# A gated transformer block on one core: first FFN product between values and scores, the weight fold inside layer one, batch two's input by transposes, second FFN matrix quantised after the RELU low halves

## The chip, the cores and the metric

The kernel runs on one core of one Trainium2 chip. The metric is the device time of one execution in microseconds (us).

## The reference, cut to what matters

```python
xn = _layernorm(x, axis=-1)                   # x: 8 batches x 512 rows x 256 columns
# attention branch
q, k, v = (gelu(xn @ W1 + b1) @ W2 + b2 for each of q, k, v)
scores = einsum('bid,bjd->bij', q, k) / sqrt(256 * 512) * tril
s = layernorm(einsum('bij,bjd->bid', scores, v)) * ln_w + ln_b
# ternary FFN branch
Wq = clip(round(W / (mean(abs(W)) + EPS)), -1, 1)         # for both matrices
g = silu(relu(xn @ Wq1.T + b1) @ Wq2.T + b2)              # 256 -> 1024 -> 256
out = x + s * g
```

## The kernel before

One program per engine, each with its order written out by hand and joined by semaphores. Every engine runs eight batches: batch 0 as straight code with the preparation woven in (`first=True`), batches 1 to 6 mostly as a hardware loop, the last as straight code again. So the places named below are a position in an engine's list, and a wait on one engine holds everything behind it on that engine.

Each fp32 product is made of fp32r products of a high half and a low half: ACT rounds a tile to its high half, DVE (for v POOL) subtracts it from the full value and so makes the low half, and PE multiplies hi by hi, lo by hi and hi by lo. For GELU and RELU, ACT applies the function twice, once into the high half and once in place in PSUM (lines 423/424 and 441/442), and DVE subtracts (`g_lo`, line 594, and `r_lo`, line 670).

PE's order in a batch:
- layer one, six products of 6 matmuls (`ORDER`), from the transposed normalised input `xT`;
- K: z = the folded matrix W2q W2k applied to gelu(k), two products;
- V: four groups of matmuls of 256 columns;
- D: one product of two matmuls with `e`, which makes a per-row term `d` that enters the scores; DVE reads it with four instructions (line 647);
- F1: the FFN's first matrix, eight products of 4 matmuls;
- S: the scores, four products;
- Y0 (tiles 0 and 1) and Y1 (tile 2): the second FFN matrix, which needs all eight `r_lo` (`r_split`);
- O: scores times v; Y2 (tile 3); then the next batch.

Y0, Y1, O and Y2 are called so below; K(i) is the first K product of batch i. The PSUM banks are used in a ring: the table `AT_...` gives each result its place, place modulo 8 is the bank, and `claim` makes PE wait until the result eight places earlier has been read.

DVE's order in a batch behind the r_lo: scale the scores (`s_scale`) and make their low halves, `xT_lo` of the next batch, add the bias to Y0 and Y1, statistics of the batch after next (`x_statistics`, batches 0 to 5 only), `o_scale(0)` (line 687), bias of Y2, `o_scale(1)`, two `finish`, then of the next batch the two `e` steps and `g_lo(0)`, `g_lo(1)`, on which K waits. POOL has, between the two o_scale, `offset(0)` (line 353, behind o_scale(0)) and in its queue behind that the reciprocal root `o_rstd_of(1)` (line 347), for which o_scale(1) waits.

Preparation in batch 0. Two matrices are folded on PE (`fold_weights(0)`, `(1)`), two fp32 matmuls each of 257 columns. The first matrix of the FFN is quantised by DVE in two halves (`quantise1`), the second five eighths by DVE (`quantise2`, two instructions, lines 548 and 550) and the rest by POOL (`quantise_rest`). The input of batch 0 is normalised by DVE and transposed on PE (`transpose_x0`, eight transposes). Batch 1 and all later ones come by DMA from a transposed copy of x, with mean and reciprocal root spread over the partitions by a round trip through DRAM (`load_xT`, `spread_x_norm`), and POOL centres and scales them (`xT_centre`, `xT_scale`).

Of the kernel before, what the change touches and what calls it, by code (L numbers as in the profile page):

```python
# [9 lines left out]
P = 128  # L10
# [13 lines left out]
AT_L1, AT_K, AT_V, AT_D, AT_F1, AT_S, AT_Y0, AT_Y1, AT_O, AT_Y2 = 0, 6, 8, 10, 11, 19, 23, 24, 25, 29  # L24
# [3 lines left out]
AT_X0 = 2  # L28
# [9 lines left out]
def gated_block(nc, x, x_t, x_norm_rows, w_qkv, w1t, w2t, cols, rows, out):  # L38
# [13 lines left out]
    with ctx:  # L52
# [3 lines left out]
        def sem(name):  # L56
# [87 lines left out]
        b2q_beside, wq_hi_made, wq_split, wv_hi_made, wv_split, bias_read = (  # L144
            sem("b2q_beside"), sem("wq_hi_made"), sem("wq_split"), sem("wv_hi_made"), sem("wv_split"),
            sem("bias_read"))
# [41 lines left out]
        def _(sp):  # L188
# [20 lines left out]
            def spread_x_norm(b):  # L209
# [3 lines left out]
                sp.wait_ge(x_norm_stored, 16 * b)  # L213
# [3 lines left out]
            load_xT(1)  # L217
            spread_x_norm(1)
# [28 lines left out]
        def _(pool):  # L247
# [35 lines left out]
            x_rstd_of(1)  # L283
            pool.wait_ge(v_shift_made, CK + 1)
# [27 lines left out]
            def xT_scale(b, k):  # L312

                half = xT32[:, k].rearrange("q (t p) -> q t p", t=TT)
                pool.wait_ge(xT_centred, CK * (b - 1) + k + 1)
                nc.gpsimd.tensor_tensor(half, half, x_rstd_all, ALU.mult).then_inc(xT_normalised, 1)  # L316

            def batch(i, first=False, second_last=False, last=False):
                if not last:
                    pool.wait_ge(xT_loaded, 16 * (i + 1))  # L320
                    pool.wait_ge(x_norm_loaded, 16 * (i + 1))
                if first:
                    pool.wait_ge(w1_quantized, 1)
                    xT_centre(0)
# [3 lines left out]
                elif not last:  # L328
                    for k in range(CK):
# [43 lines left out]
        def _(act):  # L373
# [26 lines left out]
            def xT_hi(b):  # L400
                act.wait_ge(f1_summed, 8 * b)
                for k in range(CK):
                    act.wait_ge(xT_normalised, CK * (b - 1) + k + 1)
# [12 lines left out]
            fold_hi(0)  # L416

            def batch(i, first=False, last=False):
                for p, m in enumerate(ORDER):
# [15 lines left out]
                for f in range(FT):  # L435
# [14 lines left out]
                if not last:  # L450
# [22 lines left out]
                squares(1)  # L473
# [456 lines left out]
```

## Time and profile before

| | us |
|---|---|
| median of three runs | 317.12 (317.08 to 318.56) |
| profiled execution, its own time | 320.86 |
| its span in the profile | 319.1 |
| PE busy | 308.5 (97%) |
| DVE busy | 248.9 (78%) |
| ACT busy | 220.4 (69%) |
| POOL busy | 138.7 (43%) |

The profiled execution is 3.7 us longer than the median of the runs, and 1.8 us of it lie outside the span. PE is busy nearly throughout, so the few places where it waits and the speed at which it starts are what to read; the shares of the other engines say little.

### The profile page before, as it was taken

The page shows a single profiled execution, that of the slowest core. Times are in us where ns is not written, and L with a number is a line of the kernel's source. Part 1 is how long each engine was busy: PE and PEld are TensorE (multiplying, and loading weights), DVE is VectorE, ACT ScalarE, POOL GpSimd, SP SyncE. Part 2 cuts the span into 40 slices and gives each one's busy share as a digit, 9 for nine tenths or more (in the row PEclk, how much of TensorE's full clock was granted, in tenths as well). Part 3 has the DMA queues.
Part 4 walks back from the last instruction along what each step waited for, and adds up shares of the span by engine and source line. Part 5 has one row for each costly group of instructions (what it writes and reads, how often), then busy time and mean ns, then how long its engine had stood idle before and what let it go on. Part 6 is the DMA issues. An engine that isn't in the chain of part 4 may idle for free.

```text
span 319.1 us, 5626 instructions
## 1 busy us (share of the span) xinstructions
PE 308.5 (97%) x1842; PEld 274.8 (86%) x1842; DVE 248.9 (78%) x544; ACT 220.4 (69%) x416; POOL 138.7 (43%) x105
## 2 busy tenths in 40 slices
PE   7999979899999999999999999999999999999994
PEld 7888879688998889888998889988898889988894
DVE  4688999895879769795879768796797868597677
ACT  3395927929579486867669494885868586694952
POOL 3652773529142670609433390517516192322200
PEclk9999999999999999999999999999999999999999
DMA  7962034230003100050003200050001400010001
GB/s 249 382 207 87 0 119 147 71 129 0 1 3 132 66 0 0 31 166 0 0 0 116 82 0 0 0 177 21 0 0 43 154 0 0 0 66 2 1 3 66
DMA packets 15772, 20.11 MB, mean 63 GB/s; under 512 B 1936, under 2 KB 12688, under 8 KB 15760
## 3 DMA queue, kind: packets, MB, share of 16 engines
q1 hardware_dynamic: 15056, 19.04, 18.2%
q10 hardware_dynamic: 704, 0.93, 0.8%
q8 instruction: 6, 0.10, 0.1%
q14 instruction: 6, 0.05, 0.1%
HBM read 15.74 MB, written 4.22 MB: 63 GB/s over the span
## 4 chain that ended last, share of the span: by engine, by line
PE 85%; DVE 8%; ACT 3%; issue 2%; POOL 1%; DVEq 0%; POOLq 0%; ACTq 0%
PE bank L775 83%; DVE s_lo L665 2%; PE bank L767 1%; ACT r_hi L441 1%; ACT bank L442 1%; DVE gw L687 1%; DVE gw L702 1%; PE bank L760 1%; POOL o_rstd L347 0%; DVE x_all L704 0%; DVE x_stats L511 0%; DVE r_lo L670 0%; POOL gw L353 0%; DVE y L693 0%; DVE gw L723 0%
## 5 line engine op out<-in xcount | busy, mean ns | idle before, releaser
L670 DVE TENSOR_TENSOR r_lo<-bank,r_hi 128x512 fp32r<-128x512 f32 x64 | 43.8, 691 | 29.5 <-ACT bank L442 29.4
L441 ACT ACTIVATE r_hi<-bank,col 128x512 fp32r<-128x512 f32 x64 | 47.1, 736 | 28.2 <-PE bank L775 28.2
L310 POOL TENSOR_TENSOR y<-y,xn 128x512 f32<-128x512 f32 x14 | 23.8, 1700 | 57.6 <-DMA xn<-x_norm_rows 53.3
L442 ACT ACTIVATE bank<-bank,col 128x512 f32<-128x512 f32 x64 | 45.5, 711 | 0.0
L347 POOL TENSOR_TENSOR o_rstd<-o_var,neg_half 128x2 f32<-128x2 f32 x16 | 11.3, 704 | 69.9 <-ACT o_var L465 69.8
L775 PE MATMUL bank<-xT_lo,w1q 128*128 128x512 f32 x128 | 39.8, 392 | 0.0
L775 PE MATMUL bank<-xT_hi,w1q 128*128 128x512 f32 x128 | 39.8, 392 | 0.0
L775 PE MATMUL bank<-w2q,r_lo 128*128 128x256 f32 x256 | 35.6, 281 | 2.4 <-DVE r_lo L670 2.1
L423 ACT ACTIVATE g_hi<-bank,col 128x512 fp32r<-128x512 f32 x48 | 33.7, 703 | 3.5 <-PE bank L775 2.5
L775 PEld LDWEIGHTS bank<-w2q,r_lo 128*128 128x128 f32 x256 | 31.9, 188 | 3.4 <-DVE r_lo L670 3.3
L775 PE MATMUL bank<-w2q,r_hi 128*128 128x256 f32 x256 | 34.7, 278 | 0.0
L594 DVE TENSOR_TENSOR g_lo<-bank,g_hi 128x512 fp32r<-128x512 f32 x48 | 30.8, 682 | 2.7 <-ACT bank L424 2.7
L424 ACT ACTIVATE bank<-bank,col 128x512 f32<-128x512 f32 x48 | 32.4, 674 | 0.0
L775 PEld LDWEIGHTS bank<-w2q,r_hi 128*128 128x128 f32 x256 | 31.8, 188 | 0.0
L449 ACT CAST s_hi<-s 128x512 fp32r<-128x512 f32 (+3 forms) x32 | 14.8, 461 | 24.4 <-DVE s L658 20.7
L775 PE MATMUL bank<-xT_hi,w_hi 128*128 128x512 f32 x96 | 31.2, 406 | 0.0
L775 PE MATMUL bank<-xT_hi,w_lo 128*128 128x512 f32 x96 | 30.7, 401 | 0.0
L775 PE MATMUL bank<-xT_lo,w_hi 128*128 128x512 f32 x96 | 30.6, 401 | 0.0
L775 PEld LDWEIGHTS bank<-xT_lo,w1q 128*128 128x128 f32 x128 | 24.0, 188 | 5.4 <-DVE neg_thr L543 0.2
L775 PEld LDWEIGHTS bank<-xT_hi,w1q 128*128 128x128 f32 x128 | 24.1, 188 | 5.3
L353 POOL TENSOR_TENSOR gw<-gw,row 128x512 f32<-128x512 f32 x14 | 20.8, 1484 | 16.8 <-DVE gw L687 16.8
L316 POOL TENSOR_TENSOR y<-y,xn 128x512 f32<-128x512 f32 x14 | 23.7, 1691 | 1.0
(129 smaller groups left out, 700.3 us busy)
## 6 DMA issues: line engine op xcount, KB each, us to landing
out<-x_all SPq DMA_DIRECT2D x15, 256.0 KB, 2.2
x_all<-in_x SPq DMA_DIRECT2D x7, 512.0 KB, 3.5
y<-in_x_t SPq DMA_DIRECT2D x7, 512.0 KB, 3.8
xn<-x_norm_rows SPq DMA_DIRECT2D x7, 512.0 KB, 3.5
x_all<-in_w1t SPq DMA_DIRECT2D x1, 1024.0 KB, 9.6
x_all<-in_w2t SPq DMA_DIRECT2D x1, 1024.0 KB, 12.0
row<-in_rows ACTq DMA_DIRECT2D x1, 512.0 KB, 7.1
x_all<-in_x SPq DMA_DIRECT2D x1, 256.0 KB, 3.1
```

The source lines that it names most:

```text
L310: nc.gpsimd.tensor_tensor(half, half, x_mean_all, ALU.subtract).then_inc(xT_centred, 1)
L316: nc.gpsimd.tensor_tensor(half, half, x_rstd_all, ALU.mult).then_inc(xT_normalised, 1)
L347: nc.gpsimd.tensor_tensor(o_rstd[:, half], o_var[:, half], neg_half[:, half], ALU.pow).then_inc(o_rstd_made, 1)
L353: nc.gpsimd.tensor_tensor(gw[:, half], gw[:, half], row[:, ROW_LNB:ROW_LNB + 1].broadcast_to((P, 2, C)), ALU.add).then_inc(s_made, 1)
L423: nc.scalar.activation(g["hi"][:, m], pre[:], ACT.Gelu, bias=b1)
L424: nc.scalar.activation(pre[:], pre[:], ACT.Gelu, bias=b1).then_inc(l1_whole, 1)
L441: nc.scalar.activation(r["hi"][:, f], pre[:], ACT.Relu, bias=b1)
L442: nc.scalar.activation(pre[:], pre[:], ACT.Relu, bias=b1).then_inc(f1_whole, 1)
L449: nc.scalar.copy(s["hi"][:, at], s32[:, at]).then_inc(s_hi_made, 1)
L594: nc.vector.tensor_tensor(g["lo"][:, m], bank[(AT_L1 + p) % BANKS][:], g["hi"][:, m].bitcast(FP32), ALU.subtract).then_inc(g_split, 1)
L670: nc.vector.tensor_tensor(r["lo"][:, f], bank[(AT_F1 + f) % BANKS][:], r["hi"][:, f].bitcast(FP32), ALU.subtract).then_inc(r_split, 1)
L775: last = nc.tensor.matmul(dst, a, b, start=(n == 0), stop=(n == len(pairs) - 1))
```

## The change

Five edits.
1. Layer one starts straight behind the transposes; `fold_weights(0)` moves behind its first product and (1) behind its second. ACT's and DVE's shares of the fold move with it. The load of W1k goes ahead of that of W2k.
2. D moves from ahead of F1 to behind it, in every batch, and DVE's four reads of it from ahead of the eight r_lo to behind them. The ring's places shift: F1 takes 10 to 17, D takes 18.
3. In batch 0 `quantise2` runs behind all eight r_lo (before: between the sixth and the seventh), and ACT's rounding of v behind all eight RELU pairs (before: behind the fourth). `thresholds(1)` goes behind the z low halves.
4. Batch 1's input is no longer loaded transposed. POOL normalises it early (four `tensor_scalar`, into `xn`), PE transposes it between O and Y2 of batch 0 into banks 6 and 7, ACT rounds it between its second squares and the second SILU, and DVE makes its low half between o_scale(0) and the bias of Y2. POOL's four steps and SP's three DMAs for it go.
5. The counts of the semaphores for the later batches are lowered by one batch to match, and SP waits for the transposes before its store loop, since that loop overwrites `xn`.

```diff
-AT_L1, AT_K, AT_V, AT_D, AT_F1, AT_S, AT_Y0, AT_Y1, AT_O, AT_Y2 = 0, 6, 8, 10, 11, 19, 23, 24, 25, 29
+AT_L1, AT_K, AT_V, AT_F1, AT_D, AT_S, AT_Y0, AT_Y1, AT_O, AT_Y2 = 0, 6, 8, 10, 18, 19, 23, 24, 25, 29
...
-AT_X0 = 2
+AT_X0, AT_X1 = 2, 30
...
+            load_square(1)
             load_square(4)
-            load_square(1)
...
-            load_xT(1)
-            spread_x_norm(1)
...
+            sp.wait_ge(xT_summed, 2 * CK)
             with sp.Fori(1, B - 1) as i:
...
             x_rstd_of(1)
+            pool.wait_ge(x_rstd_made, 1)
+            pool.wait_ge(xT_summed, CK)
+            for t in range(TT):
+                nc.gpsimd.tensor_scalar(xn[:, t], x_all[:, 1, t], x_mean[:, t:t + 1], x_rstd[:, t:t + 1],
+                                        ALU.subtract, ALU.mult).then_inc(xn1_made, 1)
             pool.wait_ge(v_shift_made, CK + 1)
...
-                if first:
-                    xT_scale(1, 0)
-                    xT_centre(1)
-                    xT_scale(1, 1)
...
-            fold_hi(0)
...
                     nc.scalar.activation(pre[:], pre[:], ACT.Gelu, bias=b1).then_inc(l1_whole, 1)
+                    if first and p < CK:
+                        fold_hi(p)
                     if first and p == 1:
-                        fold_hi(1)
                         v_shifts()
...
-                    if first and f == 3:
-                        act.wait_ge(v_read, 2)
-                        nc.scalar.copy(v["hi"][:], v32[:]).then_inc(v_hi_made, 1)
+                if first:
+                    act.wait_ge(v_read, 2)
+                    nc.scalar.copy(v["hi"][:], v32[:]).then_inc(v_hi_made, 1)
...
                 squares(1)
+                if first:
+                    for k in range(CK):
+                        act.wait_ge(xT_summed, CK + k + 1)
+                        nc.scalar.copy(xT["hi"][:, k], bank[(AT_X1 + k) % BANKS][:]).then_inc(xT_hi_made, 1)
                 if not last:
                     silu(2, 2, 3 * i + 3)
...
-                dve.wait_ge(d_summed, i + 1)
-                for t in range(TT):
-                    at = slice(t * P, (t + 1) * P)
-                    nc.vector.scalar_tensor_tensor(e32[:, at], bank[AT_D % BANKS][:, at], d_const[:, 0:1],
-                                                   ident[:], ALU.add, ALU.mult, accum_out=d[:, t:t + 1]).then_inc(d_read, 1)
-                dve.wait_ge(d_read, 4 * i + 4)
...
                 for f in range(FT):
-                    if first and f == 6:
-                        quantise2()
                     r_lo(f)
                 if first:
+                    quantise2()
                     dve.wait_ge(w2_quantized, 1)
+                dve.wait_ge(d_summed, i + 1)
+                for t in range(TT):
+                    at = slice(t * P, (t + 1) * P)
+                    nc.vector.scalar_tensor_tensor(e32[:, at], bank[AT_D % BANKS][:, at], d_const[:, 0:1],
+                                                   ident[:], ALU.add, ALU.mult, accum_out=d[:, t:t + 1]).then_inc(d_read, 1)
+                dve.wait_ge(d_read, 4 * i + 4)
                 s_scale(0)
...
                     o_scale(0)
+                    if first:
+                        xT_lo(1, [bank[(AT_X1 + k) % BANKS][:] for k in range(CK)])
                     y_bias(AT_Y2, 3, 1, 3 * i + 3)
...
-                pe.wait_ge(e_split, i + 1)
-                split_product(claim(i, AT_D)[:], [(ones_r[:], e[part][:]) for part in ("lo", "hi")]).then_inc(d_summed, 1)
-
                 for f in range(FT):
...
+                pe.wait_ge(e_split, i + 1)
+                split_product(claim(i, AT_D)[:], [(ones_r[:], e[part][:]) for part in ("lo", "hi")]).then_inc(d_summed, 1)
...
                 if not last:
                     weighted_sums()
+                if first:
+                    pe.wait_ge(s_read, TT)
+                    pe.wait_ge(y_read, 1)
+                    transpose_x(xn1_made, AT_X1)
                 ffn_out(i, AT_Y2, (3,))
...
-            fold_weights(0)
             batch(0, first=True)
```

PE's list at the start, before: L760 are the transposes of batch 0, the products of 257 columns are fold_weights, the others are layer one's.

```order
L760 MATMUL bank<-ident,xn 128x128 x8
L775 MATMUL bank<-w2q_raw,raw_qkv 128x257 x2
L775 MATMUL bank<-xT_hi,w_hi 128x512 x2
L775 MATMUL bank<-xT_hi,w_lo 128x512 x2
L775 MATMUL bank<-xT_lo,w_hi 128x512 x2
```

And of the change, where line 777 is the same helper and 762 the transposes:

```order
L762 MATMUL bank<-ident,xn 128x128 x8
L777 MATMUL bank<-xT_hi,w_hi 128x512 x2
L777 MATMUL bank<-xT_hi,w_lo 128x512 x2
L777 MATMUL bank<-xT_lo,w_hi 128x512 x2
L777 MATMUL bank<-w2q_raw,raw_qkv 128x257 x2
```

The first fold has moved from the stretch in which ACT rounds the transposed input to behind layer one's first product.

DVE's list in batch 0 around quantise2 (L548 and L550), before:

```order
L640 TENSOR_TENSOR v<-bank,row 128x512 x2
L647 SCALAR_TENSOR_TENSOR e,d<-bank,d_const,ident 128x128 x4
L670 TENSOR_TENSOR r_lo<-bank,r_hi 128x512 x6
L548 TENSOR_SCALAR s<-x_all,neg_thr 128x1280
L550 SCALAR_TENSOR_TENSOR w2q<-x_all,thr,s 128x1280
L670 TENSOR_TENSOR r_lo<-bank,r_hi 128x512 x2
L655 SCALAR_TENSOR_TENSOR s<-bank,d,causal 128x128
```

And of the change (L664 is r_lo, L675 the reads of D, L649 the first step of the scores):

```order
L640 TENSOR_TENSOR v<-bank,row 128x512 x2
L664 TENSOR_TENSOR r_lo<-bank,r_hi 128x512 x8
L548 TENSOR_SCALAR s<-x_all,neg_thr 128x1280
L550 SCALAR_TENSOR_TENSOR w2q<-x_all,thr,s 128x1280
L675 SCALAR_TENSOR_TENSOR e,d<-bank,d_const,ident 128x128 x4
L649 SCALAR_TENSOR_TENSOR s<-bank,d,causal 128x128
```

The quantisation and the reads of D now both stand between the last r_lo and the scores. In the loop's body of the change the reads of D stand in the same place, between r_lo and the scores:

```order
L664 TENSOR_TENSOR r_lo<-bank,r_hi 128x512
L675 SCALAR_TENSOR_TENSOR e,d<-bank,d_const,ident 128x128 x4
L677 ISA
L647 REGISTER_ALU
L649 SCALAR_TENSOR_TENSOR s<-bank,d,causal 128x128
```

where before the loop had no instruction of work there:

```order
L670 TENSOR_TENSOR r_lo<-bank,r_hi 128x512
L653 REGISTER_ALU
L655 SCALAR_TENSOR_TENSOR s<-bank,d,causal 128x128
L658 TENSOR_SCALAR s<-bank,d 128x384
L653 REGISTER_ALU
L655 SCALAR_TENSOR_TENSOR s<-bank,d,causal 128x128
```

## Rows read from the trace of the kernel before

**Rows 1.** The chain that ended last: start us, us, what. Y0 of batches 1, 6.

```profile
81.77 37.04 PE bank L775 x224
...
266.69 41.06 PE bank L775 x259
```

**Rows 2.** Waits of PE's weight loads: total us, times, longest us.

```profile
PEld bank L775 <- DVE r_lo L670: 3.3, 7, 2.2
...
PEld bank L775 <- DVE s_lo L665: 0.3, 1, 0.3
```

**Rows 3.** PE, timeline of batch 0: start us, us, what, idle before.

```profile
8.67 1.95 PE L760 MATMUL bank<-ident,xn 128*128 128x128 f32 x8
10.41 1.92 PE L775 MATMUL bank<-w2q_raw,raw_qkv 128*128 128x257 f32 x4
11.77 1.42 PE L775 MATMUL bank<-xT_hi,w_hi 128*128 128x512 f32 x2
...
14.67 0.63 PE L775 MATMUL bank<-xT_hi,w_hi 128*128 128x512 f32 x2
...
16.07 1.03 PE L775 MATMUL bank<-w2q_raw,raw_qkv 128*128 128x257 f32 x4
16.75 0.82 PE L775 MATMUL bank<-xT_hi,w_hi 128*128 128x512 f32 x2
...
29.16 0.64 PE L775 MATMUL bank<-xT_lo,w1q 128*128 128x512 f32 x2
...
42.65 1.22 PE L775 MATMUL bank<-w2q,r_lo 128*128 128x256 f32 x8 [2.07 <-DVE r_lo L670]
...
64.18 0.74 PE L775 MATMUL bank<-g_hi,w_hi 128*128 128x512 f32 x2 [1.45 <-DVE g_lo L594]
```

**Rows 4.** Windows, 10 to 20 us: busy time (x instructions), PEclk, DMA share, GB/s.

```profile
10.00:20.00 10.00, 10.00 (x37) 8.09 (x37) 7.21 (x23) 6.41 (x16) 4.73 (x5) 1.00 0.85 307
```

**Rows 5.** ACT, timeline: rounding of batch 0's input, first RELU of batches 0, 1.

```profile
10.44 1.07 ACT L410 CAST xT_hi<-bank 128x512 fp32r<-128x512 f32 x2 [2.56 <-PE bank L760]
...
30.31 0.69 ACT L441 ACTIVATE r_hi<-bank,col 128x512 fp32r<-128x512 f32 x1 [3.23 <-PE bank L775]
...
71.58 0.69 ACT L441 ACTIVATE r_hi<-bank,col 128x512 fp32r<-128x512 f32 x1 [3.59 <-PE bank L775]
```

**Rows 6.** DVE, timeline: quantise2 in batch 0; last r_lo of batch 1.

```profile
38.93 0.88 DVE L548 TENSOR_SCALAR s<-x_all,neg_thr 128x1280 f32<-128x1280 f32 x1
39.84 1.55 DVE L550 SCALAR_TENSOR_TENSOR w2q<-x_all,thr,s 128x1280 fp32r<-128x1280 f32 x1
...
80.95 0.69 DVE L670 TENSOR_TENSOR r_lo<-bank,r_hi 128x512 fp32r<-128x512 f32 x1 [0.47 <-ACT bank L442]
```

**Rows 7.** POOL, timeline of batch 0: v's weights centred (first), low half (last).

```profile
19.11 1.85 POOL L286 TENSOR_SCALAR raw_qkv<-raw_qkv,small 128x256 f32<-128x256 f32 x2 [3.41 <-ACT o_square L397]
...
22.62 1.30 POOL L293 TENSOR_TENSOR w_lo<-raw_qkv,w_hi 128x512 fp32r<-128x512 f32 x1
```

**Rows 8.** Windows of line 647 alone (reads of D, batch 4): length, DVE busy.

```profile
181.70:183.20 1.50, 1.17 (x8) 1.00 0.00 0
```

**Rows 9.** DVE, timeline, batch 4 into 5: o_scale(0), o_scale(1), g_lo from g_lo(1) on.

```profile
201.44 0.87 DVE L687 SCALAR_TENSOR_TENSOR gw<-bank,o_rstd,row 128x256 f32<-128x256 f32 x2
...
204.39 0.88 DVE L687 SCALAR_TENSOR_TENSOR gw<-bank,o_rstd,row 128x256 f32<-128x256 f32 x2
...
210.84 2.48 DVE L594 TENSOR_TENSOR g_lo<-bank,g_hi 128x512 fp32r<-128x512 f32 x4
```

**Rows 10.** POOL, timeline, same stretch: offset(0) and o_rstd_of(1).

```profile
202.39 1.29 POOL L353 TENSOR_TENSOR gw<-gw,row 128x512 f32<-128x512 f32 x1 [1.22 <-DVE gw L687]
203.65 0.70 POOL L347 TENSOR_TENSOR o_rstd<-o_var,neg_half 128x2 f32<-128x2 f32 x1
```

**Rows 11.** PE, timeline: K(4), K(5).

```profile
175.31 0.63 PE L775 MATMUL bank<-g_hi,w_hi 128*128 128x512 f32 x2
...
212.16 0.63 PE L775 MATMUL bank<-g_hi,w_hi 128*128 128x512 f32 x2
```

More of the change, by code:

```diff
@@ L328, in batch @@
                 elif not last:
+                    pool.wait_ge(xT_loaded, 16 * i)
+                    pool.wait_ge(x_norm_loaded, 16 * i)
                     for k in range(CK):
@@ L449, in batch @@
                     nc.scalar.copy(s["hi"][:, at], s32[:, at]).then_inc(s_hi_made, 1)
-                if not last:
+                if not (first or last):
                     xT_hi(i + 1)
@@ L508, in x_statistics @@
                 if not second:
-                    dve.wait_ge(x_norm_stored, 16 * b - 16)
+                    dve.wait_ge(xn1_made, TT)
+                    dve.wait_ge(x_norm_stored, 16 * b - 32)
                 for t in range(TT):
@@ L585, in _ @@
             x_statistics(1, second=True)
-            fold_lo(0)
             dve.wait_ge(rows_loaded, 16)
@@ L632, in batch @@
                 if first:
+                    thresholds(1)
                     dve.wait_ge(w1_quantized, 1)
@@ L707, in batch @@
                 if not last:
-                    xT_lo(i + 1, [xT32[:, k] for k in range(CK)])
-                    dve.wait_ge(xT_split, 2 * i + 4)
+                    if not first:
+                        xT_lo(i + 1, [xT32[:, k] for k in range(CK)])
+                        dve.wait_ge(xT_split, 2 * i + 4)
                     y_bias(AT_Y0, 0, 2, 3 * i + 1)
@@ L753, in claim, with transpose_x @@
                 return bank[at % BANKS]
-            def transpose_x0(tiles):
-                for t in tiles:
-                    pe.wait_ge(xn_made, t + 1)
+            def transpose_x(made, at):
+                for t in range(TT):
+                    pe.wait_ge(made, t + 1)
                     for k in range(CK):
-                        last = nc.tensor.transpose(bank[AT_X0 + k][:, t * P:(t + 1) * P],
+                        last = nc.tensor.transpose(bank[(at + k) % BANKS][:, t * P:(t + 1) * P],
                                                    xn[:, t, k * P:(k + 1) * P], ident[:])
@@ L811, in batch @@
                 for p, m in enumerate(ORDER):
-                    if first and p == 2:
-                        fold_weights(1)
+                    if first and p == 1:
+                        pe.wait_ge(qkv_loaded[4], 16)
+                        pe.wait_ge(b2q_beside, 1)
+                    if first and p in (1, 2):
+                        fold_weights(p - 1)
                     if first and p % 2 == 0:
@@ L846, in batch @@
                     sum_partitions(1, abs2_summed)
-                    pe.wait_ge(ones_rounded, 1)
-                pe.wait_ge(e_split, i + 1)
-                split_product(claim(i, AT_D)[:], [(ones_r[:], e[part][:]) for part in ("lo", "hi")]).then_inc(d_summed, 1)
                 for f in range(FT):
-                    if first and f == 0:
+                    if first and f == 1:
                         pe.wait_ge(thr_made, 4)
@@ L884, in batch @@
                     weighted_sums()
+                if first:
+                    pe.wait_ge(s_read, TT)
+                    pe.wait_ge(y_read, 1)
+                    transpose_x(xn1_made, AT_X1)
                 ffn_out(i, AT_Y2, (3,))
@@ L889, in _ @@
             fold_biases()
-            transpose_x0(range(TT))
-            pe.wait_ge(qkv_loaded[4], 16)
-            pe.wait_ge(b2q_beside, 1)
-            fold_weights(0)
+            transpose_x(xn_made, AT_X0)
             batch(0, first=True)
```

20 lines of the change are left out of this document (8 added, 12 removed).

## The prediction

> **What bounds the kernel now.** I read the chain of work first. From Y0 of batch 1 to Y0 of batch 6 it is PE alone, five turns in 184.92, 36.98 each [rows 1]. So in the loop only PE's work and its short waits count. Then the waits: PE's weight loads wait for `r_lo` seven times, 3.3 in all, the longest 2.2 [rows 2]; that one is batch 0's, the other six are 1.1, so 0.18 per batch, at Y0. After a wait the first pair of matmuls takes 0.74 instead of 0.63 [rows 3, 11], so such a stop costs 0.3. Then the timeline of batch 0, where PE waits 2.07 ahead of Y0 and 1.45 ahead of K(1) [rows 3]. Together 2.07 + 1.45 + 7 x 0.3 = 5.6 are there to be had. What matters is which of these waits go and which get another cause.
>
> **The front.** Layer one starts at 11.77. The first fold runs from 10.41 to 11.77, 1.36; the second from 16.07 to 16.75, 0.68 [rows 3]. Layer one's first product takes 2.90 (11.77 to 14.67) and the second, the same work, 1.40 (to 16.07) [rows 3]. The first fold is hidden now: ACT rounds the input until 10.44 + 1.07 = 11.51 [rows 5], and layer one can't start ahead of that. Without the fold it starts at 11.6, 0.17 earlier. The fold then stands in line behind the first product, and costs 0.68 at full pace. Sum of edit 1: +0.51, if the pace rises when it did. The swap of two equal loads and the fold's moved steps on ACT and DVE I cost at nothing: they stand where these engines wait for layer one's next product anyhow; if they didn't, each would push ACT or DVE back by its own length, less than one fold on PE (0.68).
>
> **F1 in batch 0.** F1 now starts behind V: 29.16 + 0.51 - 0.47 for D (two matmuls of 512 columns, a third of 1.40) = 29.2. ACT starts its RELUs 1.15 after F1, as at 30.31 [rows 5], so at 30.35. With v's rounding out of their way the way to the last `r_lo` is batch 1's, 80.95 - 71.58 = 9.37 [rows 5, 6]: it starts at 39.7 and ends at 40.4. Now quantise2 comes, which takes from 38.93 to 39.84 + 1.55 = 41.39, 2.46 [rows 6]. Y0 needs it, so Y0 starts at 42.9, where it started at 42.65 [rows 3]: +0.25. The wait of 2.07 isn't removed; quantise2 is late in place of `r_lo`.
>
> **Batch 1's input.** Eight transposes come on PE's path. Eight took 1.74 at half pace (8.67 to 10.41) [rows 3]; bounds 0.87 and 1.74, I take 0.9, since PE is at full pace there. POOL's four steps for it (line 310 and 316's kind) go, and with them, I take it, the 0.3 for which PE waited for `s_lo` [rows 2], whose maker shared the time with them. By the Trainium skill, TensorE: Matmul & The Clock Gate, Part 4 (PE-mode transpose), transposes don't engage the full clock. Going by that they would cost 1.74 and the total would be 0.8 higher; no row of before has a transpose at full pace.
>
> K(1) stood at 64.18 with 1.45 of wait, so PE alone would have been there at 62.73. Now 62.73 + 0.25 + 0.9 - 0.3 = 63.6. DVE must be done by then: from o_scale(1) to the end of g_lo(1) are 210.84 + 0.69 - 204.39 = 7.1 [rows 9]. Six products of 1.40 ahead of K(1) put the end of Y2 at 55.2, o_scale(1) follows its bias at about 56.0 and g_lo(1) is done at 63.1, 0.5 ahead of K(1). So this wait goes, and K(1) gains 0.6.
>
> POOL normalises batch 1 in four steps ahead of centring v's weights. Two such steps of one operand took 1.85, and POOL stood idle 3.41 ahead of them [rows 7]; four at 0.93 are 3.7, so v's weights are ready 0.3 later than 22.62 + 1.30 = 23.9 [rows 7]. V's 24 matmuls of 256 columns, each half of 0.235, stand with D (0.47) ahead of F1, so V starts at about 29.16 - 0.6 - 2.8 = 25.7, and with the change 26.2: nothing. With two operands a step may take up to double: 3.7 more, of which 2.0 are covered, +1.7. I take the lower value, since the data are the same size.
>
> **The loop.** Moving D gives `r_lo` 0.47 more time ahead of Y0, which is more than 0.3: the stop at Y0 goes in all seven batches. But DVE's four reads of D, 1.17 [rows 8], were made where DVE waits for ACT, and now stand behind the last `r_lo`, where DVE is the late one. The scores' scaling starts 1.17 + 0.05 - 0.47 = 0.75 later. From there to o_scale(0) DVE's list has no hole that would take it up. Behind o_scale(0), at 201.44, comes POOL: offset(0) at 202.39, o_rstd_of(1) right behind it from 203.65 to 204.35, and o_scale(1) at 204.39 starts on that [rows 9, 10]. So it passes whole into g_lo(1), which ended at 210.84 + 0.69 + 0.05 = 211.58 and is asked for by K(5) at 212.16 [rows 9, 11]: room 0.58. The turn from K(4) to K(5) was 36.85 [rows 11]. Through DVE and POOL the new turn takes 36.85 - 0.58 + 0.75 = 37.0, with PE's restart 37.1, where PE alone could do 36.55 to 36.7. Five turns that hold statistics are 5 x 37.1 - 0.1 = 185.4 against 184.9: +0.5. The seventh has no statistics ahead of o_scale(0), so PE bounds it again: -0.3, and -0.3 for the stop at the last Y0.
>
> **Sum.** -0.6 (K(1)) + 0.5 (loop) - 0.6 (last two batches) = -0.7. That is against the profiled execution, 319.1 of span and 1.8 around it; its own time is 3.7 above the median of the runs, and I apply the same -0.7 to the median: **316.4**. This kernel's runs tell a change of 0.5% (1.6 us) from none, and this is less. SP loses three transfers ahead of its other loads and waits for the transposes only where its next store is later anyhow; nothing.
>
> **Rivals.**
> A. The loop held by DVE and POOL as above: 316.4. For it: rows 9 and 10 join without a hole. Against: it rests on a room of 0.58 against 0.75 + 0.3. Chance 0.42.
> B. DVE takes up the 0.75 somewhere, and the loop goes at PE's pace: -0.6 - 7 x 0.3 = -2.7, 314.4. For it: four of five engines have idle time, and ACT's wait for the scores may be shorter than I think. Chance 0.25.
> C. Slower: the pace rises later. Now 1.36 of fp32 matmuls stand between the transposes and layer one, and it rose at 14.6; the change leaves PE empty there for 1.2. If half pace lasts through the first fold and the second product, these cost 0.68 + 1.50 more: 318.6. It decides against the kernel before from 1.4 of delay on (half of a delay is lost), and by more than 0.5% from 4.6 on. Against it: PE works without a hole from the first product on. The Trainium skill, the same page, Part 1 (The HAM clock gate), says that activity releases the half clock and that the moment varies from run to run; by it the delay would be about that of the activity, 1.2, and the cost 0.6. Chance 0.15.
> D. Batch 1's input comes late: ACT's two roundings (1.07) [rows 5] stand behind its second squares, and the transposes end only just ahead of Y2. If layer one of batch 1 waits for them whole, or POOL's four steps are the slow ones, 1.1 to 1.7 of the gain go: 317.5 to 318.1. Chance 0.12.
> The rest, 0.06, lies outside on both sides.
>
> **Numbers.** B with some of A's lower side is faster by over 0.5% (under 315.5): 0.28. C's far end and the rest give slower (over 318.7): 0.1. The range reaches from just under B to most of C and D: 314.2 to 318.3.
>
> **What would show it.** Right: PE waits at Y0 of batch 0 still about 2 us, now for `w2q`; no wait at K(1) at about 63.6; from K(2) on a wait of about 0.4 for g_lo at every K up to K(6), turns of 37.1, and none for `r_lo` at Y0. Wrong: turns of 36.6 (B); layer one's second product at 2.9 (C); a wait of PE for `xT` ahead of layer one of batch 1, or for v's weights ahead of V (D). The prediction fails most easily at the 0.75, and at the 2.46 of quantise2 if POOL's part of the quantising runs beside it.

## The result and the profile after

The changed kernel takes 320.51 us (median of 22 runs) against 317.73 for the kernel before on the same chip (22 runs): a ratio of 1.008 [1.0061, 1.0099]. I had forecast 316.4 and a range up to 318.3. It is slower, by about the size that I had given one chance in ten.

The runs of both kernels fall into groups. Of the kernel before, 11 lie at 316.96 to 317.32, 8 at 318.14 to 318.76 and 3 at 320.10 to 320.38; of the changed one, 9 at 319.25 to 319.48, 5 at 320.44 to 320.86 and 8 at 321.94 to 322.37. One of the twelve executions of the last kernel below took 505.62 us at a mean clock of 0.561, and its ratio is of the other eleven.

The profiled execution of before, on which the forecast was built, took 320.86 (span 319.1), that of the changed kernel 320.46 (span 318.7). So between these two the change gained 0.4, where I had summed -0.7. But 320.86 lies above all 22 runs of before here. If its uppermost group (320.10 to 320.38) is the kind that was profiled, it stands against the changed kernel's middle one (320.44 to 320.86), and that is a loss of 0.35 between the medians. Either is small; most of the loss lies in the other groups.

PE's timeline of batch 0 in the changed kernel (start us, us, what, idle before), to be held against [rows 3]:

```profile
8.67 1.95 PE L762 MATMUL bank<-ident,xn 128*128 128x128 f32 x8
11.57 1.22 PE L777 MATMUL bank<-xT_hi,w_hi 128*128 128x512 f32 x2 [0.95 <-ACT xT_hi L406]
...
14.29 1.21 PE L777 MATMUL bank<-w2q_raw,raw_qkv 128*128 128x257 f32 x4
15.15 0.82 PE L777 MATMUL bank<-xT_hi,w_hi 128*128 128x512 f32 x2
...
16.74 1.03 PE L777 MATMUL bank<-w2q_raw,raw_qkv 128*128 128x257 f32 x4
...
29.27 0.71 PE L777 MATMUL bank<-xT_lo,w1q 128*128 128x512 f32 x2
...
43.03 1.17 PE L777 MATMUL bank<-w2q,r_lo 128*128 128x256 f32 x8 [1.91 <-issue]
...
52.16 1.03 PE L762 MATMUL bank<-ident,xn 128*128 128x128 f32 x8
52.95 1.19 PE L777 MATMUL bank<-w2q,r_lo 128*128 128x256 f32 x8
...
63.36 0.63 PE L777 MATMUL bank<-g_hi,w_hi 128*128 128x512 f32 x2
```

Layer one starts 0.2 earlier. F1 stands at 29.27 (forecast 29.2), Y0 at 43.03 (42.9) with 1.91 of wait, K(1) at 63.36 (63.6) without one. The eight transposes of batch 1 take 0.79 (52.16 to 52.95). What Y0 waits for is on DVE, in the place of [rows 6]; the gaps ahead of each `r_lo` are of use later:

```profile
39.85 0.69 DVE L664 TENSOR_TENSOR r_lo<-bank,r_hi 128x512 fp32r<-128x512 f32 x1 [0.46 <-ACT bank L437]
40.46 0.88 DVE L548 TENSOR_SCALAR s<-x_all,neg_thr 128x1280 f32<-128x1280 f32 x1
41.37 1.55 DVE L550 SCALAR_TENSOR_TENSOR w2q<-x_all,thr,s 128x1280 fp32r<-128x1280 f32 x1
```

In the loop PE no longer waits for `r_lo` at Y0. It waits for `g_lo` at K(2) to K(6), and the turn is 37.16 where it was 36.98 [rows 1]. The waits of PE's weight loads (total us, times, longest), against [rows 2], and K(2) and K(3) in the timeline:

```profile
PEld bank L777 <- DVE g_lo L593: 3.6, 5, 0.7
```

```profile
100.43 0.74 PE L777 MATMUL bank<-g_hi,w_hi 128*128 128x512 f32 x2 [0.30 <-DVE g_lo L593]
...
137.59 0.74 PE L777 MATMUL bank<-g_hi,w_hi 128*128 128x512 f32 x2 [0.28 <-DVE g_lo L593]
```

The chain behind that is the one forecast, against [rows 9, 10]: the reads of D at 191.63, behind the last `r_lo`, and o_scale(1) waiting for POOL.

```profile
191.63 0.34 DVE L675 SCALAR_TENSOR_TENSOR e<-bank,d_const,ident 128x128 f32<-128x128 f32 x1
...
192.91 0.35 DVE L649 SCALAR_TENSOR_TENSOR s<-bank,d,causal 128x128 f32<-128x128 f32 x1
...
204.74 0.88 DVE L686 SCALAR_TENSOR_TENSOR gw<-bank,o_rstd,row 128x256 f32<-128x256 f32 x2 [1.05 <-POOL o_rstd L343]
```

One term is off, on POOL, against [rows 7]: the four steps on xn take 4.84, 1.21 each, where I had 3.7. V's weights are ready at 25.42, and V asks for them at 26.17.

```profile
15.80 4.84 POOL L286 TENSOR_SCALAR xn<-x_all,x_norm 128x256 f32<-128x256 f32 x4
20.62 1.83 POOL L290 TENSOR_SCALAR raw_qkv<-raw_qkv,small 128x256 f32<-128x256 f32 x2
...
24.12 1.30 POOL L297 TENSOR_TENSOR w_lo<-raw_qkv,w_hi 128x512 fp32r<-128x512 f32 x1
```

The one turn of the changed kernel that has no such wait at its end, from K(6) to K(7), is 36.70:

```profile
249.11 0.74 PE L777 MATMUL bank<-g_hi,w_hi 128*128 128x512 f32 x2 [0.29 <-DVE g_lo L593]
...
285.81 0.63 PE L777 MATMUL bank<-g_hi,w_hi 128*128 128x512 f32 x2
```

### The profile page after: what moved, and what is told of

It reads as the page before. It is cut to its first block, busy times and chain, and to the rows that moved or that the text cites. A ratio compares the mean times of both kernels' runs of the same rounds, so it can differ in the third digit from the quotient of the medians.

```text
span 318.7 us, 5664 instructions
## 1 busy us (share of the span) xinstructions
PE 307.7 (97%) x1850; PEld 273.7 (86%) x1850; DVE 246.6 (77%) x544; ACT 220.1 (69%) x416; POOL 136.5 (43%) x105
## 4 chain that ended last, share of the span: by engine, by line
PE 49%; DVE 17%; ACT 15%; issue 15%; POOL 2%; DVEq 1%; ACTq 0%; POOLq 0%
PE bank L777 47%; ACT r_hi L436 6%; ACT bank L437 5%; DVE gw L686 2%; DVE gw L701 2%; DVE e L675 2%; DVE x_stats L511 2%; DVE s L652 1%; PE bank L769 1%; DVE g_lo L593 1%; DVE s L649 1%; DVE e L608 1%; POOL o_rstd L343 1%; ACT s_hi L444 1%; DVE s_lo L659 1%
## 5 line engine op out<-in xcount | busy, mean ns | idle before, releaser
L664 DVE TENSOR_TENSOR r_lo<-bank,r_hi 128x512 fp32r<-128x512 f32 x64 | 44.1, 691 | 35.1 <-ACT bank L437 35.1
L314 POOL TENSOR_TENSOR y<-y,xn 128x512 f32<-128x512 f32 x12 | 20.3, 1694 | 53.5 <-DMA xn<-x_norm_rows 53.5
L777 PEld LDWEIGHTS bank<-xT_lo,w_hi 128*128 128x128 f32 x96 | 18.4, 191 | 4.5
```

The source lines that it names most:

```text
L314: nc.gpsimd.tensor_tensor(half, half, x_mean_all, ALU.subtract).then_inc(xT_centred, 1)
L664: nc.vector.tensor_tensor(r["lo"][:, f], bank[(AT_F1 + f) % BANKS][:], r["hi"][:, f].bitcast(FP32), ALU.subtract).then_inc(r_split, 1)
L777: last = nc.tensor.matmul(dst, a, b, start=(n == 0), stop=(n == len(pairs) - 1))
```

## Which part costs: the change taken apart

The first theory is FRONT: the move of the key fold (edit 1) costs, through PE's pace. Its rival is LOOP: the move of D (edit 2) costs more per turn than I had. Four kernels ran on one chip, on which the kernel before had a median of 319.07 (32 runs). The changed kernel itself was not among them, so its 1.008 is of another chip. Each ratio is against the kernel before on the same chip, with its 95% interval.

**The kernel before, unchanged**, as a scale.

> The kernel before, unchanged, for a second profile. The profiled execution of before took 320.86 us, 3.7 above its median; where do the faster ones save that? Theory FRONT (TensorE reaches its full pace earlier in them): layer one's first product (2.90 us in the first profile) takes 1.4 to 1.5 if the profile hits a fast execution, and the turns of the loop stay at 36.85 to 37.1. Theory LOOP (PE's own turn is shorter in them, which a loop held by DVE and POOL can't use): first product again 2.9, turns of 36.5 or less. Times: ratio 1.000 within 0.5%.

Measured: 319.21 us, ratio 0.9993 [0.9964, 1.0022]. Its profiled execution (span 317.4) belongs to the groups that the first profile did not show. Windows of 1 us: length, busy us of PE, PEld, DVE, ACT and POOL, PEclk, DMA share, GB/s.

```profile
8.00:9.00 1.00, 0.75 (x6) 0.40 (x6) 0.97 (x3) 0.00 (x0) 0.16 (x1) 1.00 1.08 356
9.00:10.00 1.00, 1.00 (x5) 0.82 (x5) 0.56 (x2) 0.81 (x2) 0.92 (x2) 0.62 1.11 373
10.00:11.00 1.00, 1.00 (x4) 0.76 (x3) 1.00 (x2) 0.36 (x2) 1.00 (x1) 0.50 1.05 407
...
12.00:13.00 1.00, 1.00 (x5) 0.82 (x4) 0.97 (x3) 0.00 (x0) 1.00 (x1) 0.67 1.02 418
```

Here four transposes take 0.76 (7.50), so PE is at its upper level (2.4 GHz) from about 6 us on, not from 14.6. It falls to the lower one (1.2 GHz) at about 9.2, after a stop of 0.25 between the transposes and with the fold's product just begun, and is back at 12.7. Layer one starts at 10.32, 1.4 sooner than in [rows 3]. I call this an early start, and that of [rows 3] a late one. Of before's 32 runs on this chip 27 have a mean clock of 0.991 to 0.995 and take at most 319.72 us, and 5 have 0.998 or 0.999 and take 320.75 to 321.35. Since the clock's column doesn't show the half pace of a late start, I take the 27 for executions with an early one; this is inferred from a few profiles, not seen in each run.

**The changed kernel with D back in its place.**

```diff
-AT_L1, AT_K, AT_V, AT_F1, AT_D, AT_S, ... = 0, 6, 8, 10, 18, 19, ...
+AT_L1, AT_K, AT_V, AT_D, AT_F1, AT_S, ... = 0, 6, 8, 10, 11, 19, ...
```

(with the product and the reads of D moved to match)

> The changed kernel with the D product back ahead of F1 and its four reads back ahead of the RELU low halves (edit 2 undone). Theory LOOP: the waits of PE at K(2) to K(6) (0.7 each on the weight loads) go, PE waits 0.18 for r_lo at each Y0 again, turns fall from 37.17 to at most 37.0, and the time falls by 1 to 2.5 us, to 318 to 319.5, nearly all that the change lost. Theory FRONT (the loss is in batch 0's start): turns may change, but the time stays within 0.7 us of the changed kernel's, 320.5.

Measured: 321.45, ratio 1.009 [1.0055, 1.0125].

**The changed kernel with the fold back in its place**: the load order, ACT's and DVE's steps and PE's first fold product as before.

> The changed kernel with the fold back where it was: first one ahead of layer one, second behind its second product (edit 1 undone). Theory FRONT: the time falls by 1 to 2.5 us, since PE has matmuls again between the transposes and layer one and the fold is off the path. Theory LOOP: it falls by at most 0.7, the 0.5 that the fold costs in line.

Measured: 319.45, ratio 1.002 [0.9997, 1.0044].

**The kernel before with the move of D alone.**

> The kernel before with edit 2 alone: the D product behind F1 and its reads behind the RELU low halves, in every batch. Theory LOOP: turns of 37.1 to 37.2 with waits for g_lo at K(2) to K(6), and 1 to 2.5 us slower than before, 319 to 320. Theory FRONT: within 0.7 us of before. My forecast's own sum for this edit was 0.1 to 0.2 less than before.

Measured: 319.32, ratio 1.0011 [0.9982, 1.004].

LOOP falls as the cause of the loss. The `g_lo` waits are there with the move of D and gone without it, but taking it back gains nothing here. The intervals of these two ratios, 0.3% to each side, still leave room for some tenths of a us. FRONT stands: without the fold's move three quarters of the loss are gone (1.002 for 1.008, each with an interval of 0.2%). Edits 3 and 4 were not run alone; with edit 2 they make up that 1.002, which is not clear of 1. The profile of the kernel with the fold back also shows a new wait. Its PE is fast in front, reaches V early and finds v's weights late, behind POOL's steps on xn:

```profile
25.00 0.50 PE L778 MATMUL bank<-w_hi,g_hi 128*128 128x256 f32 x2 [2.08 <-POOL w_lo L297]
```

## Why the fold's move costs

These four ran on a chip with the kernel before at 318.19 (35 runs).

**The kernel before with the fold's move alone.**

```diff
             transpose_x0(range(TT))
-            pe.wait_ge(qkv_loaded[4], 16)
-            pe.wait_ge(b2q_beside, 1)
-            fold_weights(0)
...
-                    if first and p == 2:
-                        fold_weights(1)
+                    if first and p in (1, 2):
+                        fold_weights(p - 1)
```

(with ACT's and DVE's steps and the order of the two loads moved as in edit 1)

> The kernel before with the move of the key fold alone (load order, ACT's and DVE's fold steps, PE's fold product of half 0 from ahead of layer one to behind its first product). FRONT (the fold's move is the loss): its ratio to the kernel before is that of the whole change, 1.006 to 1.010, and layer one starts near 10.2 with TensorE idle about 1 us ahead of it, the granted clock falling to half for about 3 us behind that gap in many executions. TOGETHER (the fold's move costs only with the transposes of batch 1 or the later quantise2 beside it): ratio 0.998 to 1.003. SPREAD (each part costs a third): 1.002 to 1.004.

Measured: 320.46, ratio 1.0059 [1.0032, 1.0086]. Edit 1 alone carries most of the loss. The swap of the two loads was not run apart from it.

**The changed kernel with four idle products in the gap.**

```diff
             transpose_x(xn_made, AT_X0)
+            for _ in range(4):
+                nc.tensor.matmul(bank[7][:, 0:P], ones[:], ident[:], start=True, stop=True)
```

> The changed kernel with four idle products (ones by the identity, 128 columns, into bank 7, read by nobody) on TensorE between the transposes of batch 0 and layer one, where the key fold's half 0 stood before; the fold stays behind the first product. It computes the same. CLOCK (the loss is the clock that falls in the idle 1 us ahead of layer one): the executions with a clock of 0.983 to 0.995 become rare and the median falls by 1.0 to 2.0 us, to a ratio of 1.001 to 1.004 against before. LINE (the loss is the fold standing in line, 0.68 at full pace, and what it pushes): no change, 1.007 to 1.010. LATE (at half pace four such products take 1.7 against an idle 0.95, so layer one starts later): slower still, 1.010 to 1.012.

Measured: 318.85, ratio 1.0041 [1.0013, 1.0069]. Against the changed kernel's 1.008 work that does nothing took back half of the loss, 0.39% or 1.2 us; the two ratios are of different chips, and their difference has an interval of 0.34% to each side. Its profiled execution is the same as that of the changed kernel down to 10.41, so the two can be held side by side:

```profile
8.68 1.95 PE L762 MATMUL bank<-ident,xn 128*128 128x128 f32 x8
10.41 1.61 PE L902 MATMUL bank<-ident,ones 128*128 128x128 f32 x8
11.78 0.71 PE L777 MATMUL bank<-xT_hi,w_hi 128*128 128x512 f32 x2
...
13.26 1.03 PE L777 MATMUL bank<-w2q_raw,raw_qkv 128*128 128x257 f32 x4
...
22.01 0.63 PE L777 MATMUL bank<-g_hi,w_hi 128*128 128x512 f32 x2
...
25.69 0.51 PE L777 MATMUL bank<-w_hi,g_hi 128*128 128x256 f32 x2 [0.60 <-POOL w_lo L297]
...
42.57 1.15 PE L777 MATMUL bank<-w2q,r_lo 128*128 128x256 f32 x8 [1.67 <-issue]
```

Layer one starts 0.21 later (11.78 for 11.57), but its first product takes 1.48 where the changed kernel's took 2.72, and K(0) comes at 22.01 instead of 23.23. So PE came to full pace before 11.8 with the gap filled and at about 15 without. This pair of late starts doesn't show that the filling did it: in [rows 3] the fold kept PE at work over the same gap, and the pace rose at 14.6. Of the 1.22 won, 0.60 go to the wait for v's weights and Y0 comes 0.46 earlier.

**The same with eight more ahead of Y0**, where PE waits for quantise2.

```diff
                 if first:
+                    for _ in range(8):
+                        nc.tensor.matmul(claim(i, AT_Y0)[:, 0:P], ones[:], ident[:], start=True, stop=True)
                     pe.wait_ge(w2_quantized, 1)
```

> As the one with idle products in front, and eight more of them in batch 0 ahead of the first tile of Y, where TensorE waits 1.9 to 2.4 us for quantise2; into bank 7, which that tile then starts afresh. TWO FALLS (the clock falls a second time behind that wait in some executions, as it did at 44.3 to 47.6 in the run with D moved back): 1.2 to 1.6 us less in those executions, no cluster with a clock of 0.983 left, a further 0.001 to 0.004 of ratio. ONE FALL: same as the run before it within 0.0015.

Measured: 319.41, ratio 1.004 [1.0014, 1.0066]: nothing more. The changed kernel has its uppermost group at a mean clock of 0.983; with the front filled no execution of either kernel was under 0.989, so that group was already gone, and I can't say what the second filling would have done for it.

Its profiled execution has an early start, and the filled gap didn't keep the clock up. It fell at 8.7, behind a stop of 0.24, and was back at 12.1:

```profile
8.00:9.00 1.00, 0.76 (x5) 0.55 (x5) 1.00 (x3) 0.00 (x0) 0.33 (x1) 0.85 0.97 328
...
12.00:13.00 1.00, 1.00 (x5) 0.77 (x5) 0.96 (x5) 0.00 (x0) 0.96 (x1) 0.94 0.98 385
```

So what the filling changes in such an execution is not whether the clock falls but how soon it is back; it is set against the unfilled kernel below.

**The fold back, and POOL's four steps on xn behind the split of v's weights.**

> The changed kernel with the fold where it was before and POOL's four steps on batch 1's xn (4.8 us together) moved behind the split of v's weights. XN IN THE WAY (these steps make V wait 2.1 us when the front is fast): V does not wait, F1 starts 1.5 to 2 us earlier, and the median falls by 0.8 to 1.8 us, below the kernel before (ratio 0.995 to 0.999). HELD BY QUANTISE2 (the 2.1 goes over into the wait ahead of the first tile of Y, since DVE's chain of thresholds and quantise steps ends at the same time): V's wait gone but Y at 41.5 or later, ratio 1.000 to 1.003 as without the move.

Measured: 319.14, ratio 1.0011 [0.9985, 1.0037], against 1.002 without it. V's wait of 2.08 is gone, and F1 is early. Y0 comes at 39.86, where it came at 41.86 without the move, sooner than HELD BY QUANTISE2 had it. But it still waits 1.67 for quantise2, and in the profiled execution the clock is at half behind that wait for some 3 us, from 40.3 on. K(1) comes at 61.91 against 62.33: of the 2.1 taken off the path little is left.

**Three more profiles of the changed kernel itself**, since its one profile was of the middle group. They are of another chip, with the kernel before at 319.23 (17 runs).

> The changed kernel as it is, once more, for its profile. The one profile of it so far is of an execution whose TensorE came to full pace late, at 15. GIVES BACK (an execution that comes to full pace at 6 to 7 loses the clock ahead of layer one and again behind the wait ahead of the first tile of Y): layer one starts near 10.2 to 10.6, half pace from about 9 to 13.6 and from about 44 to 47.6, Y of batch 0 at 42.5 to 43.1 as in the late one, span 320.2. ONE FALL: half pace only in front, span 317.5. NEITHER: another stretch of half pace, or a longer turn than 37.17 in the loop.

> As the look before it: a second execution of the changed kernel. GIVES BACK, ONE FALL and NEITHER expect the same as there; a span of 318.7 with layer one at 11.57 would be the late start again.

> As the two looks before it, a third execution of the changed kernel, with the same three expectations; if all three looks and the first profile show the same front to 10.4 and differ behind it, the differing stretches in the clock's column account for all of the difference between their spans to within 0.3.

Measured: spans 322.0, 320.3 and 319.0 (times 323.76, 322.12 and 320.82). The third is the late start again. The second has the time and the mean clock (0.983) of the changed kernel's uppermost group, and it shows the lost clock; PE's timeline and the windows of 1 us:

```profile
7.30 0.77 PE L762 MATMUL bank<-ident,xn 128*128 128x128 f32 x4
8.31 0.76 PE L762 MATMUL bank<-ident,xn 128*128 128x128 f32 x4 [0.24 <-DVE xn L528]
10.12 1.22 PE L777 MATMUL bank<-xT_hi,w_hi 128*128 128x512 f32 x2 [1.05 <-ACT xT_hi L406]
...
12.85 1.92 PE L777 MATMUL bank<-w2q_raw,raw_qkv 128*128 128x257 f32 x4
14.20 1.42 PE L777 MATMUL bank<-xT_hi,w_hi 128*128 128x512 f32 x2
...
42.91 1.71 PE L777 MATMUL bank<-w2q,r_lo 128*128 128x256 f32 x8 [1.89 <-issue]
```

```profile
9.00:10.00 1.00, 0.07 (x1) 0.00 (x0) 0.56 (x2) 1.00 (x2) 0.92 (x2) 0.58 1.07 377
...
15.00:16.00 1.00, 1.00 (x4) 0.81 (x3) 0.66 (x3) 0.17 (x1) 1.00 (x2) 0.50 1.09 362
16.00:17.00 1.00, 1.00 (x6) 0.84 (x5) 1.00 (x2) 0.18 (x1) 1.00 (x1) 1.00 1.10 350
...
44.00:45.00 1.00, 1.00 (x6) 1.00 (x6) 0.96 (x5) 0.04 (x1) 1.00 (x1) 0.50 0.56 147
45.00:46.00 1.00, 1.00 (x7) 1.00 (x6) 0.96 (x3) 0.97 (x2) 0.27 (x1) 0.50 1.00 353
```

The clock is at half from about 9.2 to 16.0 and again from 43.3 to 46.7, behind the wait ahead of Y0. It falls where it fell in the execution of before, with PE busy 0.75 and 0.76 of the 1 us ahead; but there, with the fold at work, it was back at 12.7, and here, with PE empty for 1.05, at 16.0. That is 3.3 later, half of it lost: 1.6 (an estimate). The first product, the first fold and the second product take 2.73, 1.35 and 2.42 where they take 1.40, 0.68 and 1.40 at full pace: 3.0 us. The first two halves of Y0 (42.91 to 46.13) take 3.22, against 1.91 in the first profile of the changed kernel (43.03 to 44.94): 1.3 more. GIVES BACK holds in both falls, with the first one 2.4 longer than it had: PE starts layer one at 10.12, yet Y0 comes at 42.91, as in the late start. In the execution of before with an early start Y0 comes at 40.93 and K(1) at 62.54; here K(1) comes at 64.78. That is 2.2 of the 2.9 between the two spans, and the turns (37.20 here) make up the rest.

The profile with both gaps filled is the nearest partner of this one: the same kernel but for the idle products, an early start, a fall behind the same stop of 0.24. There the clock was back at 12.1 and not at 16.0. K(0) came at 21.58 and not at 23.11, K(1) at 62.32 and not at 64.78, and the span is 317.8 and not 320.3. So 1.5 of the 2.5 stand in front, and the rest behind Y0, where the clock didn't fall with that gap filled. Over all the profiles in which PE had reached its upper level before the gap (at about 6 to 8): with the fold in it the clock fell in one of seven and was back at 12.7; with the gap empty it fell in all three, and was back at 16.0, 15.5 and, in the kernel with D back, at 13.6; filled, it fell in the one there is, and was back at 12.1. So an empty gap goes with the long stretch in two executions of three, and what makes the third shorter is open.

The first of the three profiles has a late start and both stretches, half pace up to about 17.7 and again from 44.8 to 48.2. Its gap is the one of the first profile of the changed kernel, where the pace rose at 15, so the moment of the rise varies by itself too. The half pace at its start is not in the clock's column, as it was not in [rows 4]. So the column can't account for the spans, as was expected of it: the first and the third profile, both late starts, differ by 3.0, of which the half pace behind Y0, 3.4 long, makes about 1.7 (an estimate). The group of the changed kernel at 319.25 to 319.48, mean clock 0.993 to 0.995, has no profile.

## A version that beats both

Y0's wait stood in every profile of both kernels. DVE ends late at it, and yet sits idle ahead of four `r_lo`, 0.46 each in the changed kernel. The next four kernels ran on a chip with the kernel before at 317.95 (35 runs).

**Woven**: the kernel with the fold back and xn later, with quantise2 in two pieces between the low halves and one more slab of the matrix on POOL.

```diff
-        FQ = 5
+        FQ = 4
...
                 for f in range(FT):
+                    if first and f in (4, 6):
+                        quantise2((4, 6).index(f))
                     r_lo(f)
-                if first:
-                    quantise2()
```

> The changed kernel with the fold where it was before, POOL's steps on xn behind the split of v's weights, and the second FFN matrix quantised on DVE in two pieces in gaps of the RELU low halves (the flags ahead of the fifth, the second step ahead of the seventh, where DVE sits idle 0.34 to 0.47 four times), with one more of its eight slabs on POOL (idle 4.1 us behind its own three). DVE THE BOUND (quantise2's 2.4 us behind r_lo is all that TensorE waits for ahead of the first tile of Y in batch 0): that wait of 1.7 is gone, Y starts near 38.1 to 38.5, and with no idle stretch the clock has nothing to fall behind there: the median falls by 1.7 to 3.0 us against the run with xn later, ratio to before 0.991 to 0.996. POOL THE BOUND (its fourth slab, 2.1 us more, ends near 38 and v_lo of 2.4 behind it near 40.5): the wait goes over to Y or to the weighted sums, ratio 0.998 to 1.002.

Measured: 317.48, ratio 0.9984 [0.9958, 1.0009], not clear of 1. The wait at Y0 shrank from 1.67 to 0.59, now for POOL, and the clock did not fall up to there in its profiled execution (span 314.9). DVE THE BOUND was right that the wait shrinks, and expected too much of it; the ratio is the one of POOL THE BOUND.

**Woven, with D back.**

> The woven kernel with D back where it was before (product ahead of F1, reads ahead of the RELU low halves). LOOP (edit 2 holds the turns by 0.19 each, 37.17 against 36.98): the g_lo waits are gone, K(2) to K(6) at 36.98, and the median 0.7 to 1.2 us below the woven kernel's. DVE FULL (the four D reads, 1.2 us, no longer fit between the RELU low halves in batch 0): TensorE waits 0.4 to 1.2 for r_lo ahead of Y, which eats it: 0 to +0.4 against the woven kernel, or +1.5 where the clock falls behind that wait.

Measured: 318.28, ratio 1.0016 [0.9985, 1.0047]. The chain shows five turns of 36.83 to 36.86 from start to start, of which three rows stand here: 0.3 a turn less than with D moved. They still hold short waits for `r_lo` (1.0 over six Y0). But `neg_thr` and `r_lo` now cost PE 1.0 and 1.5 in batch 0. Both mechanisms are there, and they cancel in the profiled spans (315.0 and 314.9); the median is 0.8 above, inside the intervals.

```profile
78.44 36.82 PE bank L785 x224
115.30 36.80 PE bank L785 x224
152.13 36.80 PE bank L785 x224
```

**The kernel before with only the two pieces woven in.**

> The kernel before with nothing changed but the two pieces of quantise2 (ahead of the fifth and the seventh RELU low half instead of both ahead of the seventh). DVE THE BOUND: DVE does the same work without its gaps, so the 2.07 to 2.20 wait for r_lo ahead of Y in batch 0 shrinks to 0.4 to 1.0, ratio 0.995 to 0.998. NOTHING (K(1) of batch 1 waits 1.45 for batch 1's input and takes back what Y gained): ratio 0.999 to 1.001, with K(1)'s wait grown to 2 to 3 us.

Measured: 318.52, ratio 1.0017 [0.998, 1.0054]. A miss, and neither theory named the cause. Y0's wait grew to 2.85. DVE's and POOL's timelines:

```profile
36.96 2.37 DVE L565 TENSOR_SCALAR s<-x_all,neg_thr 128x1280 f32<-128x1280 f32 x1
```

```profile
36.79 1.85 POOL L304 TENSOR_TENSOR w2q<-w2q,gw 128x768 fp32r<-128x768 f32 x1
```

The flags (quantise2's first step) take 0.88 alone [rows 6] and 2.37 here, where a POOL step had begun 0.17 before. They end 0.69 behind that step's end, so they stood for most of it.

**Woven, with the fold moved as in the change.**

> The woven kernel with the fold moved as the change has it: the price of edit 1 once nothing else waits in batch 0. CLOCK AND LINE: 1.8 to 3 us above the woven kernel (0.68 in line and 1.2 or more of half pace behind the idle 1 us ahead of layer one), ratio to before about 1.000 to 1.002. LINE ALONE: 0.5 to 0.9 above it.

Measured: 318.13, ratio 1.002 [0.9995, 1.0046]: 0.65 above the woven kernel in the median, as LINE ALONE has it, 0.36% or 1.1 us above it by the ratios, between the two expectations. The profiled execution has half pace from 8.6 to 15.5, and its span is 2.6 above the woven kernel's, as CLOCK AND LINE has it; but its mean clock of 0.987 is the lowest of the twelve runs (up to 1.0). The intervals don't part the two.

**Woven, with five slabs on DVE as in both kernels.** Another chip, before at 319.23 (17 runs).

> The woven kernel with five of the eight slabs on DVE as in both kernels, three on POOL. POOL LATE (the 0.6 that TensorE still waited for POOL's last step on the second matrix came of its fourth slab and of DVE's second step, which held that POOL step from 2.48 to 3.31): POOL is done by 36, DVE's last RELU low half by 38.6, and TensorE waits 0 to 0.3 ahead of Y: 0.3 to 0.6 less than the woven kernel, ratio 0.995 to 0.998. BLOCKED (a DVE step that meets a POOL step waits for its end, as the flags did in the kernel before with the pieces woven in, 2.37 instead of 0.88): DVE's second step takes 1.8 to 2.5 instead of 1.55, and the wait stays at 0.6 to 1.3, now for r_lo: 0 to +0.7.

Measured: 317.12, ratio 0.9942 [0.9911, 0.9974]. It is faster than the kernel before by 0.6%, and faster than the changed one by more (1.008 on its chip). Part of the 0.6% may be the chip's: the two woven kernels take nearly the same time on the two chips, and the kernel before takes 1.3 more on this one. BLOCKED was right on the mechanism: DVE's second step takes 2.72 instead of 1.55 beside POOL's, and PE waits 0.77 for `r_lo`.

```profile
35.35 2.72 DVE L569 SCALAR_TENSOR_TENSOR w2q<-x_all,thr,s 128x1280 fp32r<-128x1280 f32 x1
```

```profile
31.91 2.82 POOL L305 TENSOR_SCALAR w2q<-x_all,thr 128x768 fp32r<-128x768 f32 x1
34.88 1.85 POOL L308 TENSOR_TENSOR w2q<-w2q,gw 128x768 fp32r<-128x768 f32 x1
```

Whether it beats the woven kernel (317.48 on another chip, profiled spans 315.3 and 314.9) isn't settled.

## Why the prediction was wrong

- **The front, +0.51 for edit 1: the step that failed.** It said "if the pace rises when it did". In the profiled execution it rose at 15 instead of 14.6, and the term held. In most executions, as far as their mean clocks tell, the pace is full from about 6 to 8, and there the fold's product had kept PE busy over ACT's rounding of the input. Without it PE is empty for 1.05, and half pace, once there, holds to 16.0 in the second profile instead of 12.7. Edit 1 alone, forecast at +0.51, measured 1.0059, that is 1.9 us. Idle products in the gap took back 1.2 us of the 2.5, with an interval of 1.1 to each side. What is left between the filled kernel and the one with the fold back, 0.21%, has the size of my 0.68 for the fold in line, but its interval is 0.37% to each side, so that part isn't shown.
- **Rival C**, "the pace rises later", was the nearest one: full pace 3.3 later, though by a fall in an early start and a late return, which the one profile did not show, and not by a late first rise. I gave it 0.15 and took the rise of that profile for the usual one. The three runs listed beside it, of which the median lay 3.7 below it, should have told me that it wasn't.
- **F1, Y0 and K(1) in batch 0.** Right: F1, Y0 and K(1) within 0.25 of the forecast, quantise2 late in place of `r_lo`. What I left out is that such a wait can be followed by half pace (1.3 us and more in the second of the three profiles).
- **The transposes, 0.9.** They took 0.79. The Trainium skill, TensorE: Matmul & The Clock Gate, Part 4 (PE-mode transpose), says that transposes don't engage the full clock. By that they would have cost the 1.74 of [rows 3]; here they had it.
- **POOL's four steps.** Mis-sized: 4.84 for 3.7. At no cost in the late start, 0.60 of wait at V with the gap filled, 2.08 with the fold back. That is rival D's slow POOL, and with the steps moved it came to 0.1%, inside the interval.
- **The loop.** Right: waits of 0.3 for `g_lo` at K(2) to K(6), turns of 37.16 (37.1 forecast). Rival B falls. The turn of PE alone, K(6) to K(7), is 36.70 (36.55 to 36.7 forecast).
- **The sum.** -0.7 for the profiled execution, -0.4 measured between the two profiles. By parts: K(1) 0.8 earlier (64.18 to 63.36; forecast 0.6), the five turns behind it 0.7 longer (0.5), and the stretch from K(6) on 0.3 shorter, where I had 0.6. That last term was twice its size. Applying a sum worked out from a late start to a median of runs of another kind was the larger error.

## What to carry to other kernels

A profile is one execution. If its time lies apart from the median, find what sets it apart before costing an edit, or cost the edit in both. Work on TensorE that "stands where it waits anyway" is not free to move when it is what keeps the clock up: count the idle stretch that it leaves, and what follows it at 1.2 GHz. When an engine is the late one and has gaps, weave the late work into them, but look at what POOL does at that moment.

## What the runs showed of the hardware

- **TensorE's clock in short stops.** In the second of the three profiles of the changed kernel it fell from 2.4 to 1.2 GHz at 9.2, when PE had stopped for 0.24 and just stopped again, and once more after a stop of 1.9 ahead of Y0; in the first profile of the changed kernel it did not fall behind the same wait of 1.91. In the woven kernel, with the same stop of 0.24 at 8.2, it did not fall in front either. A stop of 1.9 is thus sometimes followed by half pace and sometimes not, in the same program. What decides it isn't settled. The Trainium skill, TensorE: Matmul & The Clock Gate, Part 1 (The HAM clock gate), says that the moment at which the clock changes varies from run to run; the executions of the changed kernel here agree (full pace first reached at about 6, 15 or 18 us).
- **DVE and POOL blocking each other.** A DVE step of 0.88 took 2.37 and one of 1.55 took 2.72 when a POOL step had begun before it. In the Trainium skill, SBUF — State Buffer, the section "SBUF: two separate sides" says that DVE, in some of its operations, and GpSimd share a pair of ports, and that whichever of the two starts first holds it for its whole instruction while the other waits. The rows agree in the main: 36.79 + 1.85 = 38.64, and from there to the end of the flags at 39.33 is 0.69, a little less than the 0.88 that they take alone.
